# Attention across heads: biases as three bf16 rows, the residual added on TensorE, and the sum copied back by ScalarE

## What is computed

```python
x = x + attn_a(layernorm(x), Wqvk, Wo)        # causal attention over tokens, 16 heads of 8
x = x + ffn(layernorm(x), ...)                # 24 experts, top 2, and its own residual
x = x + attn_b(layernorm(x), Wq, bq, Wdown, bdown, Wup, bup, Wout, bout)
x = x + ffn(layernorm(x), ...)                # the same experts again
```

```python
q = x @ Wq + bq
kv = (x @ Wdown + bdown) @ Wup + bup
k, v = split(kv)                              # q and k then get the rotation below
q, k = apply_rope(q), apply_rope(k)
att = softmax(einsum('bthd,btgd->bthg', q, k) / sqrt(8))
out = einsum('bthg,btgd->bthd', att, v).reshape(B, T, D)
return out @ Wout + bout
```

## Time and profile before

| | |
|---|---|
| median of three executions | 1192.6 us (1187.8 to 1196.16) |
| the profiled execution | 1194.95 us, its span 1193.1 us |
| TensorE busy | 84% of the span |
| VectorE, ScalarE, GpSimd busy | 63%, 59%, 62% |
| mean granted clock of TensorE | 0.906 |
| third sublayer, first to last addition to `X` | 696.5 to 951.8 us |

### The profile page before, as it was taken

How to read it: one execution, slowest core, us unless ns; L and a number is a source line. 1 busy time by engine, 2 the same in 40 slices (tenths; PEclk the granted TensorE clock), 3 DMA queues, 4 the chain that set the end, 5 groups by cost and what they waited for, 6 DMA issues and landing times.

```text
span 1193.1 us, 28577 instructions
## 1 busy us (share of the span) xinstructions
PE 998.2 (84%) x9416; PEld 779.3 (65%) x9416; DVE 755.9 (63%) x2103; ACT 698.3 (59%) x2114; POOL 739.1 (62%) x1075
## 2 busy tenths in 40 slices
PE   4999999988989862999996699889898718999990
PEld 2555555545555532999996377677776618999990
DVE  3688878777778832444443578888989643444444
ACT  3578776776767741565553466667666424655550
POOL 8645475766557225565565678788998463665651
PEclk8799999999999975999999599989989858999996
DMA  9999980000000003677664999992000015767657
GB/s 338 388 389 390 346 291 9 16 13 13 9 13 18 11 14 93 179 201 203 190 196 129 348 384 389 387 358 46 17 15 18 23 60 158 196 197 199 200 156 212
DMA packets 121847, 203.12 MB, mean 170 GB/s; under 512 B 13280, under 2 KB 67224, under 8 KB 121574
## 3 DMA queue, kind: packets, MB, share of 16 engines
q1 hardware_dynamic: 107750, 182.25, 46.8%
q0 software_dynamic: 9728, 16.95, 4.2%
q10 hardware_dynamic: 4224, 2.10, 0.6%
HBM read 76.72 MB, written 127.65 MB: 171 GB/s over the span
## 4 chain that ended last, share of the span: by engine, by line
PE 38%; POOL 21%; issue 18%; DVE 12%; ACT 7%; DMA 2%; another core or an unknown queue 1%; POOLq 1%; ACTq 0%; SPq 0%; DVEq 0%
POOL rows_out L807 14%; PE bank L1006 7%; PE bank L1397 5%; PE bank L1358 5%; PE bank L1318 3%; PE bank L1339 3%; POOL SETTLE L806 3%; DVE NMP L1577 2%; POOL rows_in L663 2%; PE bank L1313 2%; PE bank L1376 2%; DVE QK L1107 2%; DMA PT<-rows_out 2%; ACT bank L1065 1%; PE bank L988 1%
## 5 line engine op out<-in xcount | busy, mean ns | idle before, releaser
L832 ACT ACTIVATE QT<-bank,B 128x128 f32<-128x128 f32 x704 | 201.2, 368 | 181.6 <-PE bank L855 102.2
L1519 ACT ACTIVATE PT<-bank 128x512 f32<-128x512 f32 x320 | 188.1, 603 | 80.5 <-PE bank L1339 79.7
L807 POOL DMA_INDIRECT rows_out<-Y,XI x176 | 175.2, 995 | 90.8 <-POOL SETTLE L806 84.4
L855 PE MATMUL bank<-XIT,PT 128*128 128x128 f32 x1408 | 191.9, 280 | 2.0 <-DVE XIT L908 1.2
L866 PE MATMUL bank<-W,QT 128*128 x1408 | 186.9, 276 | 1.4 <-ACT QT L832 1.3
L855 PEld LDWEIGHTS bank<-XIT,PT 128*128 128x128 f32 x1408 | 173.8, 195 | 5.0 <-DVE XIT L908 3.0
L950 POOL TENSOR_TENSOR PT<-PT 128x512 f32<-128x512 f32 x128 | 157.5, 1261 | 30.3 <-ACT PT L1049 29.2
L866 PEld LDWEIGHTS bank<-W,QT 128*128 128x128 f32 x1408 | 171.7, 192 | 2.0 <-issue 2.0
L663 POOL DMA_INDIRECT rows_in<-XG,POS x128 | 126.5, 988 | 48.3 <-issue 36.4
L1358 PE MATMUL bank<-KT,QT 48*128 48x384 bf16 (+3 forms) x512 | 123.8, 313 | 11.3 <-DVE NMP L1573 7.7
L913 DVE TENSOR_TENSOR YB<-bank,B2R 128x128 f32<-128x128 f32 x176 | 51.4, 292 | 121.2 <-PE bank L866 64.9
(11 more groups left out here) (209 smaller groups left out, 1980.4 us busy)
## 6 DMA issues: line engine op xcount, KB each, us to landing
rows_in<-XI SPq DMA_DIRECT2D x32, 3120.0 KB, 29.0
PT<-in_w_dram SPq DMA_DIRECT2D x176, 256.0 KB
XI<-rows_in SPq DMA_DIRECT2D x176, 65.0 KB
W<-in_w2pack_dram SPq DMA_DIRECT2D x4, 1536.0 KB
PT<-rows_out SPq DMA_DIRECT2D x24, 256.0 KB, 6.3
rows_in<-XI SPq DMA_DIRECT2D x2, 1560.0 KB
rows_out<-Y,XI POOLq DMA_INDIRECT x176
X<-in_h_dram SPq DMA_DIRECT2D x8, 256.0 KB, 5.2
```

Of the source, the lines that this page charges most:

```text
L807: pool.indirect_dma_start(out=rows_out, out_offset=bass.IndirectOffsetOnAxis(ap=XI_I[:, u, D + 1:D + 2], axis=0), in_=Y[:, u % 4, :], in_o ...
L832: a = act.activation(HT[:, u % 2, c, :], psH[u % 2][:, c * P:(c + 1) * P], ACT.Gelu, bias=B1[:, bass.ds(e * FC + c, 1)])
L855: mm = pe.matmul(psH[u % 2][:, c * P:(c + 1) * P], W1[:, u, c * P:(c + 1) * P], XIT[:, u % 2, :], start=True, stop=True)
L1519: act.activation(PT[:, m % PT_SLOTS, :], psB[m % 2][:, :], ACT.Exp, scale=float(D) ** -0.5).then_inc(exp_done, 1)
```

## The change

Each of the two biases (`bq`, `bout`) is written as a sum of three bf16 rows, made once by VectorE between `expert_tables` and `experts_dve` of phase 0. TensorE adds each of the three with a one-row bf16 product, where it had one f32 product. `project_out` gets one further f32 product, of the identity with the tile of `X`, so that `psF` holds the residual sum. ScalarE copies it back to `X` after the exponentials of its slot, and VectorE's addition is gone. TensorE waits once for the parts.

```diff
+        BQ_H = sb("BQ_H", [1, 3, D], BF16)
+        BO_H = sb("BO_H", [1, 3, D], BF16)
+        B_REST = sb("B_REST", [1, 2, D])
...
+        def bias_parts(dve):
+
+            dve.wait_ge(b_w_in, 16 * 8)
+            for i, (bias, parts) in enumerate(((BQ_B, BQ_H), (BO_B, BO_H))):
+                rest = B_REST[:, i, :]
+                dve.tensor_copy(parts[:, 0, :], bias[:, :]).then_inc(b_parts, 1)
+                dve.wait_ge(b_parts, 4 * i + 1)
+                dve.tensor_tensor(rest, bias[:, :], parts[:, 0, :], ALU.subtract).then_inc(b_parts, 1)
+                dve.wait_ge(b_parts, 4 * i + 2)
+                dve.tensor_copy(parts[:, 1, :], rest).then_inc(b_parts, 1)
+                dve.wait_ge(b_parts, 4 * i + 3)
+                dve.tensor_tensor(parts[:, 2, :], rest, parts[:, 1, :], ALU.subtract).then_inc(b_parts, 1)
...
                 pe.matmul(ps_[:, 0:D], XST[:, s % 2, :], BQ_W[:, :], start=True, stop=False)
-                pe.matmul(ps_[:, 0:D], ONER[:, :], BQ_B[:, :], start=False, stop=True)
+                for i in range(3):
+                    pe.matmul(ps_[:, 0:D], ONESB[0:1, :], BQ_H[:, i, :], start=False, stop=(i == 2))
...
                 pe.matmul(psF[:, 0:D], BWVT[:, s % 2, :], BO_W[:, :], start=True, stop=False)
-                pe.matmul(psF[:, 0:D], ONER[:, :], BO_B[:, :], start=False, stop=True).then_inc(b_o, 1)
+                for i in range(3):
+                    pe.matmul(psF[:, 0:D], ONESB[0:1, :], BO_H[:, i, :], start=False, stop=False)
+                pe.matmul(psF[:, 0:D], IDF[:, :], row_at(X, T), start=False, stop=True).then_inc(b_o, 1)
...
                 if exists(T):
                     exps(T, s)
+                if exists(T - 3):
+                    act.wait_ge(b_o, T - 2)
+                    act.activation(row_at(X, T - 3), psF[:, 0:D], ACT.Copy).then_inc(b_x, 1)
...
-                if exists(T - 3):
-                    dve.wait_ge(b_o, T - 2)
-                    dve.tensor_tensor(tile_at(X, T - 3), tile_at(X, T - 3), psF[:, 0:D], ALU.add).then_inc(b_x, 1)
...
             pe.wait_ge(b_w_in, 16 * 8)
+            pe.wait_ge(b_parts, 8)
...
             expert_tables(dve, 0)
+            bias_parts(dve)
             experts_dve(dve, 0)
```

More of the change, by code:

```diff
@@ L258, in hybrid_layer @@
         b_w_in = sem("b_w_in")
+        b_parts = sem("b_parts")
         b_const = sem("b_const")
```

## The result

The changed kernel takes 1203.08 us (median of 20 executions), the kernel before 1196.05 us on the same chip (20 executions). The ratio is 1.0062, 95% interval 1.0042 to 1.0083: slower by 7.4 us of 1196, and under the 1% that the prediction counts as a change. Measured again on another chip, it was 1.0034 (1.0000 to 1.0069). The forecast for this sum was +0.6 us. So the class is as predicted, and the sum is 3.5 to 7 us too low. The median (1203 for 1193) lies inside the whole range (1182 to 1208) and 1 us above the upper end of the prediction's own case (1184 to 1202); 3.45 us of the distance is the kernel before itself, whose median was 1196.05 us in this comparison and 1192.6 in the one that the forecast started from. The profiled execution took 1197.64 us, its span 1195.8, at a mean granted clock of 0.909.

What follows compares the result with a forecast made beforehand. In the third sublayer the chain was taken to run on TensorE, crossing briefly to ScalarE or VectorE. Terms +0.2 - 1.8 + 0.9 + 1.3 = +0.6 us gave a forecast of 1193 us, range 1182 to 1208.

Steps and rivals of the forecast that it cites:

- the class: Whole kernel: same within about 1% (12 us), chance 0.70; slower 0.18, faster 0.12.
- the prediction's own case: Whole kernel: its priced terms sum to +0.6 us, forecast 1193 us, range 1184 to 1202; chance 0.62.
- TensorE: Bias and residual products: cheaper bf16 rows save 0.21 us, the residual adds 0.22; net +0.2 us over 23 tiles.
- The three steps: TensorE from first output-bias row to L984: 1.24 us before, about 1.25 expected after; 2.05 would mean nothing overlaps.
- the f32 pace: Rival: six one-row bf16 products cost 1.04 us a tile, +9.9 us over 23 tiles; 1203 us, chance 0.08.
- without overlap: Rival: no overlap between TensorE's projections from L997 to L984, +18.6 us; 1212 us, chance 0.10.
- VectorE's addition: Removed residual addition is on the chain nine times: -1.8 us; in other tiles the wait moves to the scaling.
- ScalarE's copy: Added copy back: hidden in plain tiles, 0.14 us idle left; five exponential stretches on the chain cost +0.9 us.
- The new waits: VectorE's statistics wait for ScalarE's copy where T%4 = 2: nothing counted at T = 18, +1.3 us at T = 26 and 30.
- the statistics wait in every group: Rival: wait passed on in eight groups, copy in all tiles, 8 x 1.0 + 32 x 0.16 = +13 us; 1206, chance 0.08.
- Outside the stretch: `bias_parts`, eight small VectorE instructions, 2 to 3 us inside a 13.21 us wait for the first rows: no cost.

Runs made afterwards that it cites:

- experiment 4: Changed kernel, but VectorE adds the residual, behind its product and reciprocal; no identity product or ScalarE copy back: 1198.81 us, ratio 1.0002 to the kernel before.
- experiment 5: The changed kernel again, without edit, on another chip: 1201.26 us, ratio 1.0034 to the kernel before.
- experiment 3: Changed kernel with ScalarE's copy back moved to the head of its slot, ahead of the exponentials: 1192.81 us, ratio 0.9980 to the kernel before.
- experiment 10: Changed kernel with VectorE's statistics moved from slots with T%4 = 2 to right behind the next slot's maximum: 1196.70 us, ratio 0.9981 to the kernel before.
- experiment 7: Changed kernel with ScalarE's copy back 0.47 us later, behind the copies of query, key and value: 1207.77 us, ratio 1.0103 to the kernel before.
- experiment 1: Changed kernel with only the bf16 bias rows; VectorE adds the residual as before: 1196.52 us, ratio 0.9995 to the kernel before.
- experiment 8: As experiment 1, plus two unused f32 filler products per tile ahead of the output projection: 1188.35 us, ratio 0.9943 to the kernel before.
- 9: Kernel before, plus two unused f32 filler products per tile ahead of the output projection: 1193.91 us, ratio 0.9979 to the kernel before.
- 11: As experiment 1, plus four filler products per tile ahead of the output projection: 1193.36 us, ratio 0.9971 to the kernel before.
- 12: As experiment 3, plus two filler products per tile ahead of the output projection: 1195.17 us, ratio 0.9981 to the kernel before.
- experiment 2: Changed kernel with f32 bias products again, keeping the residual on TensorE and ScalarE's copy back: 1205.67 us, ratio 1.0070 to the kernel before.
- experiment 6: Changed kernel with VectorE's statistics moved from slots with T%4 = 2 to the end of the next slot: 1205.36 us, ratio 1.0102 to the kernel before.

## Why the prediction was right, and where it was not

**TensorE: right.** The three steps were to take 1.25 us and take 1.18. Three one-row bf16 products cost 0.27 for 0.31. The residual and L999 behind it take 703.57 - 702.93 = 0.64 us where L982 had 0.42: +0.22, as priced. At the f32 pace the two triples would have cost 1.04 us, and without overlap the three steps 2.05; both rivals are out.

**VectorE's addition: right in kind.** It waits 1.61 us at the scaling (0.17 + 1.4 was forecast), and plain slots gain nothing from it. Experiment 4 shows the same from the other side. The term of -1.8 us itself is not shown: it is smaller than what a ratio here can tell, and 0.2 us taken off the chain in experiment 4 brought no gain.

**ScalarE's copy: right.** 0.15 us of its wait for the transpose is left in a plain tile (0.14 was forecast), and the plain slot doesn't pay.

**The new waits: this step failed.** Where the wait would be, was right; so was its length at T = 18 (0.8 forecast, 0.82 measured). The prediction then said: "There the next exponentials start 0.42 us after L1110 has ended ..., and TensorE is the chain, so I count nothing." By its own numbers 0.8 is more than 0.42, so 0.4 us had to be passed on (0.49 measured, in the slots of experiment 5 where L476 is short), and a chain that runs on TensorE doesn't take that in: it crosses to VectorE as soon as the exponentials are late, as TensorE's 1.53 us of wait at 838.24 show. Nor did it see the second part, 0.54 us at T = 18, in which L476 stands behind a product of GpSimd once it is pushed past that product's start. The term of +1.3 us should have been 0.99 us in each of five groups, 0.54 in T = 6 and 0.25 to 0.5 in T = 30: about +6. This is the first term of the rival "the statistics wait in every group" (8 x 1.0), whose point of decision, more than 0.42 us, was met; its second term, 0.16 in each tile, was not. With the term corrected the sum is 0.6 - 1.3 + 6 = +5.3 us, between the two measurements (+4.1 and +7.4), and the upper bound of the term (+8) holds it, which is why the range does. That the class came out as forecast is in part luck: the loss stayed under the 12 us that count as a change, and the reason given for the small sum was wrong in this term. Experiments 3 and 10 take the wait away in two different ways, and both end at 0.998; experiment 7 enlarges it and ends at 1.010.

**Outside the stretch: right.** `bias_parts` ran from 461.50 to 463.63 us, 2.1 us for the forecast 2 to 3, and what follows it still waits 10.82 us where it waited 13.21:

```profile
461.50 0.21 DVE L950 CAST BQ_H<-BQ_B 1x128 bf16<-1x128 f32 x1
463.35 0.28 DVE L956 TENSOR_TENSOR BO_H<-B_REST,BO_H 1x128 bf16<-1x128 f32 x1
474.45 0.65 DVE L912 COPY XIT<-bank 128x128 f32<-128x128 f32 x2 [10.82 <-PE bank L853]
```

Experiments 1, 3 and 4 carry it too and end at 0.998 to 1.000 of the kernel before.

**What stays open.** The bf16 rows save 0.28 us in a plain slot and the whole shows 0.6 us, and why is not shown. A part may have gone to the clock: in all four pairs the kernel with filler had the higher mean clock, in the last within the noise (+0.0077 for experiment 8 over 1, counted against the kernel before each time, +0.0054 for 9, +0.0036 for 11 over 8, +0.0019 for 12 over 3; the standard error of each is about 0.002). Whether time follows isn't settled: it fell in the first pair (0.9995 to 0.9943, two chips, intervals that just overlap) and perhaps in the second, not in the other two, and in the third the filler was itself on the path. The rest may be blocks as the one at 832.81: among the profiled executions a call of L476 or L477 of 5.0 to 5.6 us was in experiments 2, 3, 4, 5 and 10, once in each, and in none of the others. Another small VectorE instruction of the routing, L621, took 6.22 us in experiment 4 and 8.23 us in experiment 6. Nothing was run that takes these away.

## What to carry to other kernels

An instruction that others wait for shouldn't be moved behind a long one on its new engine without following every semaphore that it counts: compare the delay with the slack of the first engine behind each waiter, and pass on what exceeds it, even where another engine holds the chain. Here the same copy cost nothing visible ahead of the exponentials and 6 to 10 us where it was put, by the ratios. And when a small instruction of VectorE is pushed in time, look at what GpSimd is doing at its new place.

## What the hardware showed that was not expected

- A VectorE instruction on 128x4 elements, 0.17 us alone, takes 0.71 or 1.24 us when it meets one of GpSimd's products, up to the end of that one, and 5.03 us in experiment 10 (5.04 in experiment 5), where it starts 0.08 us (0.10) ahead of four products in a row (4.90 us) and ends with the last of them. The rule of the Trainium skill ("SBUF — State Buffer", the same section), that the one that starts first has the lock for one instruction, would make this 0.17 us, or 1.3 at most by an estimate from one product's 1.23; the measurement decides. Why it doesn't get through between two products, no run here shows.
- One-row bf16 products keep the pace of full ones: three of them span 0.34 us, the last of it 0.21, so they start 0.06 us apart, where the full ones start 0.057 apart. With the change of shape on both sides three take 0.27 us.
- TensorE's mean granted clock was higher by 0.004 to 0.008 in three pairs where it had products that nobody needs in its waits, and by 0.002, within the noise, in the fourth. What the lower clock costs is in one row: from 838.2 to 841.6 us TensorE was granted 0.50 of its clock, the lower of its two levels (1.2 GHz), behind a wait of 1.53 us at a granted 1.00. The 16 products at 838.24 took 3.66 us there, and at the full clock they take 2.05. Whether the wait brought the lower level, these runs don't tell.
